# A two-layer graph-attention kernel: four of the eight operand chunks in two buffers instead of two, made one per row block amid the running head

## What is computed

```
Wh = einsum('nf,hfd->hnd', x, W_heads)
s1, s2 = (Wh * a1).sum(-1), (Wh * a2).sum(-1)          # per head and node
e = leaky_relu(s1[:, :, None] + s2[:, None, :], 0.2)
att = softmax(where(adj > 0, e, -9e15), axis=-1)       # 4096 x 4096 per head
hp = elu(einsum('hnm,hmd->hnd', att, Wh))              # layer 0; layer 1 has no elu
x = layernorm(x + feat @ W_out + b_out)                # layer 0
x = layernorm(x + heads side by side)                  # layer 1
```

## Time and profile before

| | |
|---|---|
| median of 3 runs | 3120.64 us (3114.76 to 3123.39) |
| span of the profiled execution | 3118.6 us |
| layer 0 attention, first to last L674 | 290.2 to 2232.5 us |
| layer 1 attention, first to last L674 | 2491.1 to about 3061 us |
| PE busy | 2780.7 us, 89% |
| DVE busy | 2232.4 us, 72% |
| ACT busy | 2114.1 us, 68% |
| POOL busy | 652.6 us, 21% |
| mean granted PE clock | 0.954 of full |

### The profile page before, as it was taken

One profiled execution on the slowest core, in us unless ns is written; L12 is line 12 of the kernel. 1 busy time (PEld: TensorE's weight loads), 2 busy tenths in 40 slices (PEclk: granted clock), 3 DMA queues, 4 the chain that ended last, 5 costly groups with the idle time before them and its releaser, 6 DMA issues. The chain is left out here.

```text
span 3118.6 us, 76790 instructions
## 1 busy us (share of the span) xinstructions
PE 2780.7 (89%) x27212; PEld 2406.7 (77%) x27212; DVE 2232.4 (72%) x4443; ACT 2114.1 (68%) x3536; POOL 652.6 (21%) x586
## 2 busy tenths in 40 slices
PE   6885999899899899899899899899797589889892
PEld 4553888788788788788788788788686488889892
DVE  6677757756856856865865866855444599999997
ACT  3554776777678687677678687677411379889892
POOL 0003303402501600610620520500011123141400
PEclk9997999999999999999999999999898899999996
DMA  8994111101101101100100110100253311111115
GB/s 303 367 373 156 30 23 29 37 17 35 30 23 33 33 23 29 38 23 16 44 23 23 30 37 23 29 24 16 85 172 119 108 32 29 35 30 34 30 27 165
DMA packets 214904, 213.28 MB, mean 68 GB/s; under 512 B 67905, under 2 KB 177601, under 8 KB 214818
## 3 DMA queue, kind: packets, MB, share of 16 engines
q1 hardware_dynamic: 214818, 212.07, 21.9%
HBM read 161.09 MB, written 50.93 MB: 68 GB/s over the span
## 5 line engine op out<-in xcount | busy, mean ns | idle before, releaser
L674 PE MATMUL l0a_ps<-l0a_uv,l0a_b 128*128 128x258 f16 x8192 | 1848.7, 274 | 114.0 <-DVE l0a_b L783 94.2
L674 PE MATMUL l0a_ps<-l0a_uv,l0a_c 128*128 128x258 f16 x8192 | 1848.2, 275 | 0.0
L711 ACT ACTIVATE l0a_b<-l0a_s1b,l0a_kcur 128x512 fp8e4<-128x512 f32 x2048 | 1288.6, 708 | 191.4 <-PE l0a_ps L674 179.3
L674 PEld LDWEIGHTS l0a_ps<-l0a_uv,l0a_b 128*128 128x128 fp8e4 x8192 | 806.6, 98 | 242.0 <-issue 120.2
L674 PEld LDWEIGHTS l0a_ps<-l0a_uv,l0a_c 128*128 128x128 fp8e4 x8192 | 795.9, 97 | 123.9
L781 DVE SCALAR_TENSOR_TENSOR l0a_c<-l0a_b,mask_t 128x512 uint32<-128x512 uint32 x512 | 446.9, 873 | 484.2 <-ACT l0a_b L711 484.2
L674 PE MATMUL l1a_ps<-l1a_uv,l1a_b 128*128 128x130 f16 x4096 | 514.0, 223 | 45.7 <-DVE l1a_b L783 35.7
L674 PE MATMUL l1a_ps<-l1a_uv,l1a_c 128*128 128x130 f16 x4096 | 514.5, 225 | 0.0
L711 ACT ACTIVATE l1a_b<-l1a_s1b,l1a_kcur 128x512 fp8e4<-128x512 f32 x768 | 477.2, 714 | 47.1 <-DMA l1a_ncur<-l_ncol 43.3
L674 PEld LDWEIGHTS l1a_ps<-l1a_uv,l1a_b 128*128 128x128 fp8e4 x4096 | 410.5, 100 | 51.1 <-issue 50.4
L783 DVE TENSOR_TENSOR l0a_b<-l0a_b,mask_t 128x512 uint32<-128x512 uint32 x512 | 449.3, 878 | 0.0
(11 more groups left out here) (160 smaller groups left out, 2178.1 us busy)
## 6 DMA issues: line engine op xcount, KB each, us to landing
l0p_raw<-in_adj SPq DMA_DIRECT2D x128, 512.0 KB, 6.1
l_wh<-l0p_whs SPq DMA_DIRECT2D x32, 512.0 KB, 6.5
l0a_s1b<-l_srow SPq DMA_DIRECT2D x64, 256.0 KB, 3.3
l0a_whx<-l_wh SPq DMA_DIRECT2D x64, 256.0 KB, 3.5
feat<-l0a_ob SPq DMA_DIRECT2D x64, 256.0 KB, 2.4
pj_fin<-feat SPq DMA_DIRECT2D x32, 512.0 KB, 5.2
l1a_s1b<-l_srow SPq DMA_DIRECT2D x32, 256.0 KB, 2.9
l0p_xin<-in_x SPq DMA_DIRECT2D x32, 128.0 KB, 6.2
```

What stands on the lines that cost most here:

```text
L674: last = nc.tensor.matmul(sums(q, t, m), buf[k % nbuf][:, j, t * P:(t + 1) * P], row[:, 2 * m * W1:2 * (m + 1) * W1], start=first and sets ...
L711: last = act.activation(bbuf[k % nbuf][:, j, :], s1b[q][:, :], ACT.Relu, bias=kcur[q][:, jt:jt + 1], scale=STEEP, saturate=False)
```

## The change

- Four chunks (`TWIN = 4`: 0 to 3) have two places in `uv` instead of two.
- `MAKE` is 0 to 7, the order in which a head's first block uses the chunks.
- POOL's wait for chunk c below 4 is now for the end of block 1 + c of the running head, so these chunks are released at the starts of blocks 2, 3, 4 and 5 (counted from 0), one at each. Before, chunks 0 and 1 waited only for the head before the running one, and in effect for their loads. Chunks 4 to 7 wait, as before, until PE's last block has used them.
- SP issues the second four loads in the last block but one.
- To make room in SBUF, `e1`, `vt` and `mt` are one tile: `vt` and `mt` are views into `e1`, the fold works in place, and ACT's L735 waits for the result of the block before (`s_out`) instead of for its folds (`s_dv`). Layer 0 no longer has `ncur`, which it did not use.

```diff
-MAKE = [0, 1, 7, 6, 2, 3, 4, 5]
+MAKE = list(range(CPB))
+TWIN = 4
...
-        uv = s.sb("uv", [P, (CPB + 2) * JC, 4 * W1], F16)
+        uv = s.sb("uv", [P, (CPB + TWIN) * JC, 4 * W1], F16)
...
-        e1 = [s.sb(f"e1{t}", [P, 2 * W1], F32) for t in range(TPB)]
-        vt = s.sb("vt", [P, TPB, W1], F32)
-        mt = s.sb("mt", [P, TPB, D], F32)
+        e1 = s.sb("e1", [P, TPB, 2 * W1], F32)
+        vt, mt = e1[:, :, 0:W1], e1[:, :, W1:W1 + D]
...
-            return (CPB + c if par and c < 2 else c) * JC
+            return (CPB + c if par and c < TWIN else c) * JC
...
-                    pool.wait_ge(s_pe, PE_OFFSET + HC * h - (HC if c < 2 else c))
+                    pool.wait_ge(s_pe, PE_OFFSET + HC * h - (HC - CPB * (2 + c) if c < TWIN else c))
...
-                    if b == NB - 1 and not last:
+                    if b == NB - 2 and not last:
...
-                act.activation(mt[:, :, :], mt[:, :, :], ACT.Exp).then_inc(s_ex, 1)
+                act.activation(mt, mt, ACT.Exp).then_inc(s_ex, 1)
...
-                    act.wait_ge(s_dv, g * links + t + 1)
-                    act.mul(e1[t][:, :], sums(q, t, 0), column("sb", g * TPB + t)).then_inc(s_e1, 1)
+                    act.wait_ge(s_out, g + 1)
+                    act.mul(e1[:, t, :], sums(q, t, 0), column("sb", g * TPB + t)).then_inc(s_e1, 1)
...
-                    dve.tensor_tensor(vt[:, t, :], e1[t][:, 0:W1], e1[t][:, W1:2 * W1], ALU.add).then_inc(s_dv, 1)
+                    dve.tensor_tensor(vt[:, t, :], vt[:, t, :], e1[:, t, W1:2 * W1], ALU.add).then_inc(s_dv, 1)
```

More of the change, by code:

```diff
@@ L511, in attention_phase @@
         kcur = [s.sb(f"kcur{q}", [P, NT], F32) for q in range(2)]
-        ncur = [s.sb(f"ncur{q}", [P, NT], F32) for q in range(2)]
+        ncur = [s.sb(f"ncur{q}", [P, NT], F32) for q in range(2)] if dve_tiles else []
         mnb = [s.sb(f"mnb{q}", [P, D], F32) for q in range(2)]
@@ L607, in load_block @@
                              ).then_inc(s_blk[q], 16)
-                for tile, name in ((kcur, "kcol"), (ncur, "ncol"))[:2 if dve_tiles else 1]:
+                for tile, name in ((kcur, "kcol"),) + (((ncur, "ncol"),) if dve_tiles else ()):
                     sp.dma_start(tile[q][:, :], d[name].rearrange("h p t -> p h t")[:, bass.ds(h, 1), :].rearrange(
@@ L792, in evacuate @@
                     dve.wait_ge(s_e1, n + 1)
-                    dve.scalar_tensor_tensor(e1[t][:, :], sums(q, t, 1), column("sc", n), e1[t][:, :],
+                    dve.scalar_tensor_tensor(e1[:, t, :], sums(q, t, 1), column("sc", n), e1[:, t, :],
                                              ALU.mult, ALU.add).then_inc(s_ev, 1)
@@ L835, in add_exponentials @@
                 dve.wait_ge(s_st, 16 * g)
-                dve.scalar_tensor_tensor(ob[:, :, :], mt[:, :, :], -1.0, vt[:, :, 0:D],
+                dve.scalar_tensor_tensor(ob[:, :, :], mt, -1.0, vt[:, :, 0:D],
                                          ALU.add, ALU.add).then_inc(s_out, 1)
```

## The result

The changed kernel takes 3240.11 us (median of 4 runs, 3236.84 to 3246.62), the kernel before 3122.01 beside it (3114.76 to 3124.41). The ratio is 1.0383, with a 95% interval of [1.0364, 1.0402]: 3.8% slower. The profiled execution's span is 3239.2 us against 3118.6, so 120.6 us are to be found.

What follows compares the result with a forecast made beforehand. PE was taken to be bound by DVE's chain at block starts, slowed by turns with POOL. Terms 95 + 34 - 14 - 4 = 111 us on 3118.6 gave 3230 profiled, 3231 by median; range 3168 to 3275.

Steps and rivals of the forecast that it cites:

- What bounds it: Layer 0's attention: PE stalls because POOL slows DVE's chain by taking turns, not because `uv` is late.
- The twins, 95 us: Blocks 2 to 5 of seven heads: 28 edge releases delay DVE's chain, PE stalling 3.4 us each, 95 us.
- the first rival's mechanism: At twin edges, one DVE instruction slips through where POOL waits for its own semaphore; 3184 us, chance 0.18.
- The clock, 34 us: After the 28 pauses: PE's clock falls in four of five at 1.5 us, 1.2 each, 34 us.
- The head changes, -14 us: Seven head changes: four chunks left, shorter stalls and no late pause in the last block, 14 us gained.
- First blocks, -4 us: First blocks of head 0, both layers: two chunks instead of three follow POOL's last, 4 us gained (0 to 6).
- Layer 1, 0 us: Layer 1's attention: chunk count stays; spreading may lose up to 10 us or save up to 10, taken as 0.
- The merged tile, 0 us: Exponential and L836 read rows in four pieces, up to 3 us; L735's new wait is met earlier; taken as nothing.
- Strictly in turn: Rival at twin edges: no overlap, chain 5.3 us late, 4.4 us stalls, 147 us more, 3268 us; chance 0.12.
- the same, smaller: Rival at twin edges: chain 3.4 us late, 2.4 us stalls, clock seldom falls, 63 us more, 3184 us; chance 0.18.
- Faster: Rival: POOL misses the chain, starting over 5 us after the edge or finishing early at head changes; 3035 us, chance 0.06.
- the second rival's count: At twin edges, without overlap, five POOL instructions of 1.05 us between DVE's own, 5.3 us late; 3268 us, chance 0.12.

Runs made afterwards that it cites:

- the last run with ACT's old wait: Changed kernel with twin chunks released three chunks into their blocks and ScalarE's old wait added back before each of four multiplies: 3109.33 us, ratio 0.9969.
- the first experiment: Changed kernel with each of the four twin chunks released three chunks into its block instead of at the edge: 3112.33 us, ratio 0.996.
- the fastest kernel: Changed kernel with DVE's splits and ACT's compares moved earlier in layer 0 and four SyncE loads issued a block later: 3072.02 us, ratio 0.9848.
- the combined kernel: Changed kernel with DVE's splits and ACT's compares moved earlier and twin chunks released three chunks into their blocks: 3213.79 us, ratio 1.0294.

## Why the prediction was right, point by point

- **What bounds it** held. The kernel went from 37 to 9 waits for L783 when POOL's work left the block edges, with nothing else changed.
- **The twins, 95 us.** The 28 pauses are 3.3 us each, 92.9 us together, before position 2 and released by L783. Five instructions of the chain were held, as counted, but not the five that were named. The first fold was ready 0.1 us before the end of POOL's first instruction and slipped through in 0.28 us; the prediction has it ready "during the second", though by its own numbers (508.31 against 507.3 + 1.05 = 508.35) it is during the first. The first L815 slipped through in 0.34 us as POOL waited for its own semaphore, which was the first rival's mechanism. The second and third L815 were held in their place, since POOL ran to 7.0 us into the block. The end of L824 came 8.3 us into the block instead of 4.3, so 4.0 us late and not 4.3, and 0.15 us more lies between the mask of position 2 and its matmul, where the prediction had nothing. The mechanism held; that two slips left the count at five and the pause at 3.3 for 3.4 is partly luck.
- **The clock, 34 us.** 133.7 - 92.9 = 41 us, 1.5 per pause and not 1.2. The clock fell behind 21 pauses of 28, about as assumed, but a fall cost 1.6 us (blocks of 33.5) and 2.7 in block 2 of heads 1 to 6 (34.7), where I had 1.5.
- **The head changes, -14 us.** 95.3 to 79.5 is -15.8. The pause of 1.0 us is gone from all seven last blocks, 7 us as forecast, and the first blocks give the other 9, a little more than the 7 forecast. The first block of head 1 still takes 39.9 us. With the release off the edge 12.1 us are left of the gain, and 11.7 in the last run with ACT's old wait; what made the other 4 in the changed kernel was not followed. But the reason given for the 7 us, fewer chunks, is not the only one that does it: with six chunks and the new wait the same pauses go.
- **First blocks, -4 us.** Only 0.9 us in layer 0 (45.1 to 44.3) and 0.8 in layer 1. This term was mis-sized, in its part for the clock. The work after POOL's last chunk of head 0, now and before (PE's row between them is the matmul that starts it now):

```profile
328.40:338.30 9.90, 9.88 (x64) 7.64 (x65) 4.09 (x9) 1.43 (x3) 0.00 (x0) 0.71 0.00 0
```

```profile
328.42 0.37 PE L674 MATMUL l0a_ps<-l0a_uv,l0a_b 128*128 128x258 f16 x1 [7.80 <-POOL l0a_uv L590]
```

```profile
324.60:335.30 10.70, 10.67 (x96) 9.33 (x97) 4.27 (x9) 3.95 (x8) 0.00 (x0) 1.00 0.01 2
```

  Two chunks follow POOL's last now and three before, as the prediction said, which is the 3.6 us. But PE waits 7.8 us at once before them, and the two chunks then run at a mean clock of 0.71 and take 9.9 us instead of 7.15. The clock took 2.8 of the 3.6 us.
- **Layer 1, 0 us.** It was +2.0.
- **The merged tile, 0 us.** By itself that was wrong: 0.67% or 21 us in the kernel before (13 us between the profiled executions). At the head changes it adds nothing to the four chunks, so the sum stood.

The terms as measured are 92.9 + 41 - 15.8 - 0.9 in layer 0, 117, and 2 in layer 1: 119 of the 120.6 us. The prediction of 3231 is 9 us below the median: the clock cost 7 us more than forecast, the first blocks brought 3 less and layer 1 cost 2 more, while the twins cost 2 less and the head changes brought 2 more.

**The rivals.** "Strictly in turn" wanted pauses of 4.4 us and "the same, smaller" 2.4; 3.3 lies between, at the forecast's. "Faster" named its condition rightly: with POOL over 5 us behind the edge the pauses vanish, as the first experiment shows. It was the release that put the change on the other side. Its 3035 us was not reached, since it counted on nearly all of the 95 us of the head changes too, and 12 went.

The rule of the Trainium skill ("SBUF — State Buffer", section "Who interferes with whom") stands where the prediction weighed it, for instructions with two SBUF inputs: folds and L815 wait for POOL's reading instructions and not for memsets, which read no SBUF. L811 takes one tensor, so what the prediction quotes of the rule doesn't cover it, and it was held by both. That nothing overlaps isn't seen here. Strictly in turn the chain would be 5.3 us late, by the second rival's count, and it was 4.0. And beside DVE's large masking instructions (0.60 us apart when undisturbed) POOL's, of 1.05, follow each other every 1.46 us in the kernel before and not every 1.65.

## What to carry to other kernels

When GpSimd prepares data beside VectorE, ask at which moment its instructions fall. Beside VectorE's large instructions with slack behind them they cost nothing here, beside a chain of small ones nearly each of them holds up one. Moving either one away took the loss in the twin blocks from 133.7 us to 0 or to 10, and moving both put them onto each other again. Follow every queue behind a moved result (here SyncE's, with four loads ahead of the inputs), since it hid a gain of 39 us. And try the parts of a change alone: the wait that came with the merged tile, costed at nothing, was worth as much at the head changes as the four chunks.

## What the runs showed that I had not expected

- A wait of ScalarE that holds nothing up, replaced by another, changes the time by 0.46% ([0.33%, 0.59%]), and not where four chunks lie at the head change. One instruction fewer in its queue moves DVE's L781 by 0.07 us, from just behind POOL's first instruction to level with it, and which of the two goes first is worth 1.0 us in each of seven blocks.
- A memset on GpSimd, which reads nothing, leaves VectorE's two-input instructions alone (56 folds and 84 L815 of 0.28 and 0.34 us) but holds the one-input L811 (0.26 to 0.56 us in 28 of 28, 0.17 alone).
- Two cures of the same stall add to a loss: 3112 and 3111 us apart, 3214 together (in the second and the third of these SyncE's queue has its share).
- Several short pauses can cost less than one. In the fastest kernel head 1's first block pauses 4.9 us in four places at a clock of 1.00, and in the changed kernel a single pause of 3.3 us leaves blocks at a mean clock of 0.95 in 15 cases of 28, 0.90 in six and 1.00 in seven. It is not so each time: a block of the combined kernel (head 1, block 4) with pauses of 2.3 and 0.7 us also has 0.95.
